# Six rows of a modulation summed in TensorE's column groups, and four VectorE sums put behind a normalisation

## What is computed

```python
mod = (_silu(L0_c) @ L0_wmod).reshape(1, 6, 1, -1)          # 1024 x 6144 weights
sa, ca, ga, sb, cb, gb = (mod[:, k] for k in range(6))
ga = (2 * (ga >= 0) - 1) * jnp.maximum(jnp.abs(ga), 0.25)    # gb likewise
h = _layernorm(x) * (1 + ca) + sa
x = x + ga * _L0_attn_ref(h, mask, weight, bias)             # one 1024x1024 product, 32x32 blocks masked
h = _layernorm(x) * (1 + cb) + sb
x = x + gb * _L0_ffn_ref(h, ...)                             # gate, up, silu, down; int weights with scales
```

## Time and profile before

| | |
|---|---|
| median of three runs | 1123.43 us (1122.3 to 1125.46) |
| span of the profiled execution | 1121.2 us |
| TensorE busy | 1087.0 us, 97% of the span |
| VectorE busy | 782.1 us, 70% |
| ScalarE, GpSimd busy | 424.0 us, 378.8 us |
| TensorE, 0 to 10 us | busy 0.08 us |
| TensorE, 104 to 112 us | busy 0 |
| DMA engines, 10 to 80 us | share 1.02 to 1.04, 387 to 409 GB/s |

### The profile page before, as it was taken

One profiled execution on the slowest core, in us unless ns is written; L12 is line 12 of the kernel. 1 busy time (PEld: TensorE's weight loads), 2 busy tenths in 40 slices (PEclk: granted clock), 3 DMA queues, 4 the chain that ended last, 5 costly groups with the idle time before them and its releaser, 6 DMA issues. The chain is left out here.

```text
span 1121.2 us, 13073 instructions
## 1 busy us (share of the span) xinstructions
PE 1087.0 (97%) x4629; PEld 513.3 (46%) x4629; DVE 782.1 (70%) x986; ACT 424.0 (38%) x776; POOL 378.8 (34%) x345
## 2 busy tenths in 40 slices
PE   5996999999999999999999999999999999999998
PEld 3553554554544444444444444444444444444444
DVE  4789967767668898888887988889544443334434
ACT  0331226646555454446555555546433000000000
POOL 1223327636665352324564565655200000000000
PEclk9998989999999999999999999999999999999999
DMA  9993212325352566346667665665289765565430
GB/s 345 404 387 83 76 38 75 105 65 182 137 205 79 168 183 184 113 122 193 179 192 209 184 185 180 194 185 176 96 325 337 259 256 232 218 246 223 183 144 37
DMA packets 130000, 206.93 MB, mean 185 GB/s; under 512 B 20624, under 2 KB 99216, under 8 KB 127504
## 3 DMA queue, kind: packets, MB, share of 16 engines
q1 hardware_dynamic: 124640, 184.08, 49.8%
q0 software_dynamic: 5296, 22.02, 5.5%
HBM read 137.39 MB, written 68.68 MB: 184 GB/s over the span
## 5 line engine op out<-in xcount | busy, mean ns | idle before, releaser
L1296 PE MATMUL pA<-work 128*128 128x512 f16 x1680 | 376.9, 379 | 3.7 <-ACT work L1036 2.0
L1296 PEld LDWEIGHTS pA<-work 128*128 128x128 f16 x1680 | 163.8, 98 | 203.9 <-ACT work L1036 4.6
L1159 PE MATMUL pA<-work 128*128 128x512 f32 x512 | 226.7, 598 | 0.7 <-issue 0.7
L1296 PE MATMUL pB<-work 128*128 128x512 f16 x752 | 175.9, 379 | 1.4 <-DVE work L1727 1.4
L1159 PEld LDWEIGHTS pA<-work 128*128 128x128 f32 x512 | 96.2, 192 | 113.0 <-issue 112.2
L1749 DVE SCALAR_TENSOR_TENSOR work<-work 128x512 f16<-128x512 f16 x144 | 122.8, 874 | 19.6 <-ACT work L1056 19.3
L1363 PE MATMUL pA<-work 128*128 128x512 f16 x600 | 134.4, 379 | 0.0
L911 ACT ACTIVATE work<-pB,small 128x128 f32<-128x128 f32 x256 | 92.7, 480 | 90.1 <-PE pB L1148 77.0
L1036 ACT ACTIVATE work<-pA 128x512 f32<-128x512 f32 x126 | 74.6, 592 | 117.3 <-PE pA L1296 112.0
L1296 PEld LDWEIGHTS pB<-work 128*128 128x128 f16 x752 | 73.5, 98 | 90.2 <-DVE work L1727 2.1
L1363 PE MATMUL pB<-work 128*128 128x512 f16 x480 | 107.5, 379 | 0.9 <-DMA work<-h_left_scratch 0.9
(11 more groups left out here) (170 smaller groups left out, 1142.1 us busy)
## 6 DMA issues: line engine op xcount, KB each, us to landing
work<-h_scratch SPq DMA_DIRECT2D x8, 4480.0 KB, 13.7
h_scratch<-work SPq DMA_DIRECT2D x60, 512.0 KB, 3.0
work<-in_L_wmod SPq DMA_DIRECT2D x10, 2048.0 KB, 17.9
work<-in_L_ffn_gate_w SPq DMA_DIRECT2D x84, 128.0 KB, 3.2
work<-in_L_ffn_up_w SPq DMA_DIRECT2D x84, 128.0 KB, 2.9
work<-down_scratch SPq DMA_DIRECT2D x7, 1280.0 KB, 12.1
work<-in_L_ffn_down_w SPq DMA_DIRECT2D x68, 128.0 KB, 2.8
work<-in_L_attn_data SPq DMA_DIRECT2D x16, 512.0 KB, 4.3
```

The source lines that it names most:

```text
L1159: last = pe.matmul(pA[:, 2 * par(t) + h, :], hT1[par(t)][:, c, :], wT[:, c, h * H:(h + 1) * H], start=(c == 0), stop=(c == KT - 1))
L1296: last = pe.matmul(ps, w[:, m, c], bc[b][:, mv_, s, c], start=begin, stop=(i == n - 1 and c == KT // 2 - 1 and s == 1), skip_group_check=True)
```

## The change

All six pieces of the first modulation (0 to 5) are now summed by `row_sum`. Each of its eight matmuls takes `csil` broadcast to 32 columns and writes one of four groups of 32 partitions of PSUM: slice t goes to group t mod 4, so that a group adds two slices. ScalarE copies 128 partitions as before, and what adds them over the partitions uses 1/32 (`share`) and 2/32 (`share2`). VectorE's sums of pieces 1, 4 and 5 are gone; its four sums of pieces 6 to 9 stay, and three of them move: that of piece 7 behind `normalise(0, 4)`, that of piece 8 behind `normalise(0, 5)` and `normalise(1, 1)`, that of piece 9 behind `normalise(0, 6)`. In SyncE's queue the loads of pieces 4 to 7 and 9 wait for other counts.

```diff
-        rowsum = [pA[:, 0, :], pA[:, 2, :], pA[:, 1, :]]
+        rowsum = [pA[:, k, :] for k in range(4)] + [pB[:, 2 + k, :] for k in range(2)]
...
             def load_piece(m):
-                if m in (4, 6):
-                    sp.wait_ge(row_summed, m // 2 - 1)
-                elif m == 5:
-                    wait_summed(sp, 1)
-                elif m == 7:
-                    sp.wait_ge(row_summed, 3)
-                elif m == 8:
+                if m == 8:
                     sp.wait_ge(mask_summed, KT)
-                elif m == 9:
-                    wait_summed(sp, 4)
+                elif m >= 4:
+                    sp.wait_ge(row_summed, 5 if m == 9 else m - 3)
...
-            for k, m in enumerate(ROWS):
-                act.wait_ge(row_summed, k + 1)
-                act.activation(acc[m // 2][:, H * (m % 2):H * (m % 2 + 1)], rowsum[k], ACT.Copy).then_inc(row_copied, 1)
+            for m in range(4):
+                copy_row(m)
...
             for u in range(KT, 2 * KT):
                 move_row_half(u)
+            copy_row(4)
+            copy_row(5)
...
-                for t in ts:
-                    last = pe.matmul(rowsum[k], csil[:, t:t + 1].to_broadcast([P, P]), w[:, t],
-                                     start=(t == 0), stop=(t == KT - 1))
+                for t in range(KT):
+                    rows = slice(Q * (t % A), Q * (t % A + 1))
+                    last = pe.matmul(rowsum[m][rows], csil[:, t:t + 1].to_broadcast([P, Q]), w[:, t],
+                                     start=(t < A), stop=(t >= KT - A))
...
-            row_sum(0)
-            columns(0, colp[:, 0:KT])
-            row_sum(1)
-            row_sum(2, range(0, 5))
+            for m in range(4):
+                row_sum(m)
+                if m % 2:
+                    columns(m // 2, colp[:, KT * (m // 2):KT * (m // 2 + 1)])
             mask_total_of(0)
-            row_sum(2, range(5, KT))
-            columns(1, colp[:, KT:2 * KT])
...
-            attend(0, 1)
             pe.wait_ge(mask_bits, 2)
             pe.wait_ge(cols1_ready, 2)
+            attend(0, 1, range(4))
+            row_sum(4)
+            row_sum(5)
+            attend(0, 1, range(4, KT))
             gate_row(2, rowp[0])
...
             dve.wait_ge(silu_c_done, 1)
-            sum_half(0, 1)
             norm1(1)
...
             mask_rows_of(1)
-            sum_half(2, 0)
             norm1(2)
-            sum_half(2, 1)
...
+            normalise(0, 4)
             sum_half(3, 1)
-            normalise(0, 4)
             residual(2)
             stats1(5)
-            sum_half(4, 0)
             normalise(0, 5)
             normalise(1, 1)
+            sum_half(4, 0)
             residual(3)
             stats1(6)
+            normalise(0, 6)
             sum_half(4, 1)
-            normalise(0, 6)
             residual(4)
             cols2()
```

More of the change, by code:

```diff
@@ L247, in adaln_kernel @@
         share = cols(1)
+        share2 = cols(1)
         bmx = cols(4)
@@ L745, in _ @@
             pool.wait_ge(consts_set, 8)
-            for v, value in ((mhalf, -0.5), (eps, EPS), (one, 1.0), (two, 2.0), (share, 1.0 / P)):
+            for v, value in ((mhalf, -0.5), (eps, EPS), (one, 1.0), (two, 2.0), (share, 1.0 / Q), (share2, 2.0 / Q)):
                 pool.memset(v, value).then_inc(consts_set, 1)
@@ L899, in _, with copy_row @@
             act.activation(csil, cvec, ACT.Silu).then_inc(silu_c_done, 1)
-            for k, m in enumerate(ROWS):
-                act.wait_ge(row_summed, k + 1)
-                act.activation(acc[m // 2][:, H * (m % 2):H * (m % 2 + 1)], rowsum[k], ACT.Copy).then_inc(row_copied, 1)
+            def copy_row(m):
+                v, h = m // 2, m % 2
+                act.wait_ge(row_summed, m + 1)
+                dst, src = acc[v][:, H * h:H * (h + 1)], rowsum[m]
+                if v == 2:
+                    act.wait_ge(acc_used, 1)
+                act.activation(dst, src, ACT.Copy).then_inc(row_copied, 1)
+            for m in range(4):
+                copy_row(m)
             act.wait_ge(acc_used, 2)
@@ L1165, in columns @@
                 if v < 2:
-                    pe.wait_ge(row_copied, 2 * v + 1)
-                    if v == 0:
-                        wait_summed(pe, 1)
-                else:
-                    for h in range(2):
-                        wait_summed(pe, 2 * v + h)
+                    pe.wait_ge(row_copied, 2 * v + 2)
+                else:
+                    pe.wait_ge(dve_summed, 4 * (v - 2))
+                rhs = share if v < 2 else one
                 for c in range(KT):
-                    rhs = share if 2 * v + c // 4 in ROWS else one
                     last = pe.matmul(dst[:, c:c + 1], acc[v][:, P * c:P * (c + 1)], rhs, start=True, stop=True)
@@ L1181, in gate_row @@
                 else:
-                    for h in range(2):
-                        wait_summed(pe, 2 * v + h)
+                    pe.wait_ge(row_copied, 2 * v + 2)
+                twice = (two if v == 5 else share2).to_broadcast([P, P])
                 for h in range(2):
-                    last = pe.matmul(dst[:, h * H:(h + 1) * H], two.to_broadcast([P, P]), acc[v][:, h * H:(h + 1) * H],
+                    last = pe.matmul(dst[:, h * H:(h + 1) * H], twice, acc[v][:, h * H:(h + 1) * H],
                                      start=True, stop=True)
@@ L1194, in mask_total_of, with row_sum @@
                   .then_inc(mask_total, 1)
[L1196 to L1200, removed]
+            def row_sum(m):
+                pe.wait_ge(piece_loaded[m], 16)
                 w = mp[m].rearrange("p (t n) -> p t n", t=KT)
-                for t in ts:
-                    last = pe.matmul(rowsum[k], csil[:, t:t + 1].to_broadcast([P, P]), w[:, t],
-                                     start=(t == 0), stop=(t == KT - 1))
-                if t == KT - 1:
-                    last.then_inc(row_summed, 1)
+                for t in range(KT):
+                    rows = slice(Q * (t % A), Q * (t % A + 1))
+                    last = pe.matmul(rowsum[m][rows], csil[:, t:t + 1].to_broadcast([P, Q]), w[:, t],
+                                     start=(t < A), stop=(t >= KT - A))
+                last.then_inc(row_summed, 1)
             def turn_rows(n):
@@ L1557, in sum_half @@
                 w = mp[m].rearrange("p (t n) -> p t n", t=KT)
-                moved = v in (3, 4)
-                dst = w[:, 0] if moved else acc[v][:, h * H:(h + 1) * H]
+                dst = w[:, 0]
                 link(dve.tensor_scalar(dst, w[:, 0], csil[:, 0:1], None, ALU.mult))
@@ L1564, in sum_half @@
                                                   op0=ALU.mult, op1=ALU.add))
[L1565 to L1569, removed]
+                by_tile = acc[v].rearrange("p (c a i) -> p a c i", c=KT, a=A)
+                parts = [(by_tile[:, 2 * h + k],) + tuple(s[:, k * KA:(k + 1) * KA].rearrange("p (c i) -> p c i", c=KT)
+                                                          for s in (w[:, KT - 1], dst)) for k in range(2)]
                 for out_, last_row, so_far in parts:
```

14 lines of the change are left out of this document (4 added, 10 removed).

## The result

The changed kernel takes 1131.64 us (median of six, 1130.84 to 1132.57), the kernel before 1123.74 in the same comparison (1122.3 to 1130.04): a ratio of 1.0056, 95% interval 1.0038 to 1.0073. The change makes the kernel slower by 0.6%, 6 to 8 us. The prediction was 1129.0 us, range 1124 to 1136, slower with a chance of 0.76.

The account below looks back on a forecast made before the run. TensorE, busy 97% of the span, was taken as the bound, tied to VectorE's closed chain. `columns` 4.3 us later plus 1.3 for the clock gave 5.6; span 1126.8, median 2.2 above it: 1129.0 us, range 1124 to 1136.

Parts of the forecast that it names:

- The place: VectorE's chain, gate row to tile 4's residual, limits the gain to 2.7 us; TensorE waits about 8 us before `columns`.
- The start of the chain: Gate row, with pieces 4 and 5 now on TensorE: ends 3.1 us later (0.9 to 5), 4.4 less 1.3.
- The earlier start: Sum of the mask through the turned rows: up to 2.5 us earlier, none at low clock; 1.3 us taken.
- The length of the chain: VectorE's waits for GpSimd's root at tiles 4, 5, 6: 7.2 us, less 3.3 returned, so 3.9 us longer (3.9 to 5.9).
- predicted return: First instructions of the sums of pieces 8 and 9 no longer meet GpSimd: 2 x 1.67 = 3.3 us back.
- The clock in `columns`: Second modulation's `columns` begin at low clock after TensorE's wait: 1.3 us more, between nothing and over 3.
- what follows: TensorE's work at the low clock before and after: about the same, up to 1 us either way.
- The sum: Whole kernel: `columns` start 4.3 us later, plus 1.3 for the clock, 5.6 us slower; 1129.0 us.
- take turns: Rival, row sums: column groups run one after another, 13.8 us for two pieces; 22 us slower, 1146; chance 0.12.
- The faster case: Rival, VectorE's chain: root ready in time, chain stays 67.2 us, `columns` start 1.8 us earlier; 1121.6 us; chance 0.07.

Follow-up runs that it names:

- e1: Changed kernel with VectorE's sums of pieces 7, 8 and 9 back at their old places ahead of the normalisations; 1126.98 us, ratio 1.0007 to the kernel before.
- e3: Changed kernel with its six row sums as matmuls of the full 128 columns instead of four column groups; 1151.58 us, ratio 1.0236 to the kernel before.
- e6: Changed kernel with pieces 4 and 5 summed and the gate row made before the last six matmuls of tile 0's attention; 1126.56 us, ratio 1.0010.
- e12: Changed kernel with VectorE summing piece 6 ahead of the gate row's clamp, while it waits for the gate row; 1126.49 us, ratio 1.0012.
- e5: Changed kernel with eight thrown-away attention products on TensorE in the wait ahead of `columns` of the second modulation; 1130.28 us, ratio 1.0035.
- e0: The kernel before, unchanged, profiled a second time; 1124.82 us in a single run, span 1123.0 us.
- e2: The kernel before with only the three moves of VectorE's sums of pieces 7, 8 and 9; 1129.55 us, ratio 1.0036.
- e4: Changed kernel with GpSimd's root for tiles 4, 5 and 6 ahead of the bias addition and store; 1130.22 us, ratio 1.0050.
- e10: Changed kernel with earlier gate row, sums 8 and 9 moved back, their first instruction a scalar_tensor_tensor; 1120.59 us, ratio 0.9949 to the kernel before.

## Why the prediction was right

**The place.** Right: the end of the closed chain on VectorE decides, and TensorE's shortened wait at tile 4 reappears at `columns` (6.90 us; about 8 predicted). Shown by e1, e3, e6 and e12, each of which moves one end or the length of the chain and moves the time with it.

**The start of the chain.** Predicted 3.1 us later, with the gate row ending near 77.6; it ended at 77.64, 3.15 later. The two terms behind it were both somewhat off. Two pieces cost 3.6 us instead of 4.4: the lower bound of 1.7 a piece was nearly met. A round of four narrow records takes 0.43 us, as long as one record of full width (13.90 us for 32), and its four loads of 0.13 us together lie within it. The earlier start was 0.6 us (54.75 against 55.38) instead of 1.3. The sum of the mask did come 1.1 us earlier (36.27 against 37.35), and from there on it was bound by VectorE's sums of the masks, which ended at 36.21 instead of 34.88. Behind it TensorE stood for 1.64 and 1.01 us and then turned the weight at a granted clock of 0.50 and 0.51, in 3.67 and 3.56 us for sixteen records each; before, 32 records took 3.87 us at 1.00. The low clock, which the prediction named as what could take this gain away, took much of it. Pieces landed later in this profile than in the first, but in e12, where TensorE did not wait for piece 0, the sum of the mask stood at 36.36 us all the same, and the turned rows at 54.30.

**The length of the chain.** Predicted waits of 0.7, 3.3 and 3.3 us, found 0.84, 3.22 and 3.22; predicted return of 1.67 us on each of two sums, found 2.15 back to 0.48. From clamp to reading the chain takes 71.7 us instead of 67.2 (148.15 + 1.22 - 77.67): 4.5 longer, where 3.9 were predicted; the other 0.6 are scattered.

**The clock in `columns`.** Predicted 1.3 us, between nothing and over 3. `columns` alone took 6.99 - 4.27 = 2.7 us more, and e5 shows that it is the clock. The row that bore on it was the transposes of the earlier trace rows that doubled from 1.91 to 3.67 us: the loads of the stationary operand are busy in all of `columns` (4.14 of 4.14 us before), as they nearly are in those transposes (3.27 of 3.67). But 1.2 us came back right behind. In the kernel before, the clock was at 0.50 from 147.4 to 153.4 us, so most of its low stretch lay behind `columns`, and from their end to L1278 it took 7.03 us (148.57 to 155.60); the changed kernel took 5.81 for the same work (156.27 to 162.08). From the start of `columns` to that point it is 11.17 us before and 12.66 now: the clock cost 1.5 us in all, near the 1.3. Here the number was partly lucky, since the prediction had put what follows at "about the same (up to 1 us either way)". In e1 and e5, whose `columns` ran at 0.98 and 0.90, the same stretch takes 9.5 and 9.6 us.

**The sum.** By the predicted terms `columns` end 5.6 us later. In the profiles the later start is 5.0 us instead of 4.3 and the clock 1.5 instead of 1.3: 6.5 us at 162 us, and the same at 860. The span is 8.2 us longer; what is missing comes at the start of the last product, above all in the wait of 1.31 us at 879.20. No term of the prediction stands for it. It is there, with 0.8 to 1.6 us, in all ten profiles of kernels that sum six pieces on TensorE, and in none of the three that sum three there (before, e0, e2), so it seems to come with the change; VectorE waits for a transfer just ahead of it, and why that comes later stays open. The median was taken 2.2 us above the span, where each run with both shows 1.8 (1131.17 against 1129.4 for the changed kernel). The medians are 7.9 us apart, the ratio of all runs says 6.3 us. 1129.0 was 2.6 us too low.

**The rivals.** The column groups do not take turns: 3.64 us against 13.90 (e3). The Trainium skill (TensorE: Matmul & The Clock Gate, Part 3) has it that a load overlaps a matmul only where its row group differs. By that rule they should have taken turns; here it does not hold for column groups, and the measurement decides. What turns would have cost was priced too low: in e3, where pieces 4 and 5 take 13.90 us together, the gate row starts 22.6 us later than before and the time is 26.5 us longer, where 22 were predicted. The faster case asked for a root in time, and it wasn't. Its reason in the prediction, that the root stands behind the bias addition, was only half of it: with the root ahead of the addition (e4) the chain was only 0.9 us shorter, because the addition itself holds VectorE up.

## What to carry to other kernels

When a wait of the busiest engine goes because work was moved on another one, follow that other engine's closed chain to the next point where the two meet: only the slack there (2.7 us here) can be won. Before a dependent instruction is put right behind its statistics, ask who computes what lies between (here GpSimd's root behind a 2.35 us addition) and what the work that is being moved away had covered. And an engine's new idle time, 15 us ahead of the gate row, is worth something when work of its own chain is pulled into it (5 us in e12), and so is an earlier date of what starts the chain (5 us in e6). What low clock a wait leaves behind is priced to the point where both kernels run at full clock again, not over the first group of instructions alone (2.7 us in `columns`, 1.5 in all).

## What the runs showed of the hardware

- Sixteen float32 matmuls of 128x512 with a stationary operand of 32 columns, written in turn to four groups of 32 partitions, take 3.64 us; sixteen of 128 columns take 13.90. That is 3.8 times faster.
- GpSimd's addition of two 128x1024 float32 tensors (2.34 to 2.35 us) holds up VectorE's next tensor_scalar (2.15 instead of 0.48; 2.76 to 2.83 instead of 0.81), and also its scalar_tensor_tensor with a broadcast second input (2.41 us, e10) and even one of 128x22 (1.92 instead of 0.18 us). VectorE's statistics, which read one tensor, are not held up: in the kernel before two of them lie wholly beside an addition and take 1.25 us, as they do without one.

```profile
230.87 2.36 POOL L766 TENSOR_TENSOR work<-work 128x1024 f32<-128x1024 f32 x1
231.30 1.25 DVE L1461 BATCH_NORM_STATS2 small<-work 128x6 f32<-128x512 f32 x2
```

- Eight `columns` of float32 128x128 by 128x1 take some 1.8 us at 2.4 GHz and 3.5 at 1.2 (3.63 and 6.99 us for sixteen).
